# Layer norm and routing of the two expert stages taken block by block

## The reference

```python
x = x + 0.5 * ffn(layernorm(x))
x = x + mixer(layernorm(x))
x = x + 0.5 * ffn(layernorm(x))
x = x + 0.5 * moe(layernorm(x))
x = x + attention(layernorm(x))
x = x + 0.5 * moe(layernorm(x))

def moe(x):                      # 64 experts of 88 hidden rows, 8 used per token
    scores = sigmoid(x @ gate_w.T)
    choice = scores + gate_bias
    # sum of the 2 best of each of 8 groups; 4 best groups; 8 best experts in them
    w = scores where chosen, divided by their sum + 1e-20, times 2.5
    routed = sum_e w[:, e] * mlp_e(x)      # mlp: silu(x Wg.T) * (x Wu.T) @ Wd.T
    return routed + shared_mlp(x)          # 2 shared experts of 88 rows
```

## Time and profile before

| | us |
|---|---|
| median of three runs (lowest, highest) | 1801.06 (1800.49, 1803.01) |
| profiled execution, device time | 1803.61 |
| profiled execution, span of the trace | 1801.8 |
| PE, DVE, ACT, POOL busy in the span | 1614.6, 1234.6, 953.1, 902.6 |
| second feed-forward, from its first matmul | 495.4 to 648.5 |
| E1 up to the first weighted expert tile, E1 from there | 648.5 to 723.8, 723.8 to 1091.8 |
| attention: layer norm and first keys, then the heads | 1091.8 to 1114.6, 1114.6 to 1353.8 |
| E2 up to the first weighted expert tile, E2 from there | 1353.8 to 1431.9, 1431.9 to 1799.1 |

### The profile page before, as it was taken

The page is one execution under the profiler, slowest core; times in us unless marked ns, Lnnn a source line. Parts: engine busy times, 40 slices in busy tenths (PEclk is TensorE's granted clock), DMA queues, the critical chain, the costliest instruction groups (busy, mean ns, idle before and its releaser), DMA issues.

```text
span 1801.8 us, 25450 instructions
## 1 busy us (share of the span) xinstructions
PE 1614.6 (90%) x6820; PEld 1208.8 (67%) x6820; DVE 1234.6 (69%) x2015; ACT 953.1 (53%) x1864; POOL 902.6 (50%) x786
## 2 busy tenths in 40 slices
PE   5999558877799985999999997999998599999998
PEld 3777323333367763788888885988885488888887
DVE  4555779999945645666666666877775466666666
ACT  3234565444434342565555564877773265655565
POOL 2000147766610023677777773344433277777776
PEclk9999779999989986999999999999997799999999
DMA  2000000000000001676777760000000366767765
GB/s 111 1 0 1 0 0 1 0 0 1 0 8 1 0 35 37 143 154 144 157 147 149 151 138 1 2 0 0 0 1 9 76 152 145 155 146 154 149 149 119
DMA packets 30035, 118.72 MB, mean 66 GB/s; under 512 B 5323, under 2 KB 17059, under 8 KB 18211
## 3 DMA queue, kind: packets, MB, share of 16 engines
q1 hardware_dynamic: 29987, 118.15, 29.8%
HBM read 116.03 MB, written 2.10 MB: 66 GB/s over the span
## 4 chain that ended last, share of the span: by engine, by line
PE 65%; DVE 3%; issue 2%; POOL 2%; ACT 2%; DMA 1%; POOLq 0%; DVEq 0%; SPq 0%; ACTq 0%
PE ps L218 18%; PE ps L220 18%; PE ps L219 18%; PE ps L1270 2%; PE ps L1255 1%; PE ps L1257 1%; PE ps L1256 1%; POOL m_hc L831 1%; PE ps L621 1%; DMA rwb<-rw_rows 1%; PE ps L240 1%; POOL e_lo L226 1%; PE ps L253 1%; PE ps L1258 1%; DMA rw_rows<-rwt 0%
## 5 line engine op out<-in xcount | busy, mean ns | idle before, releaser
L226 POOL TENSOR_TENSOR e_lo<-e_h,e_hi 128x512 fp32r<-128x512 f32 (+1 forms) x368 | 479.0, 1302 | 258.3 <-ACT e_hi L223 251.2
L1138 DVE TENSOR_TENSOR ps<-e_s,ps 128x512 f32<-128x512 f32 x352 | 245.0, 696 | 237.8 <-PE ps L220 179.1
L963 ACT ACTIVATE e_s<-ps 128x512 f32<-128x512 f32 (+1 forms) x368 | 220.2, 598 | 323.6 <-PE ps L220 323.5
L218 PE MATMUL ps<-xn_hi,eh 128*128 128x512 f32 x704 | 280.4, 398 | 22.8 <-DVE ps L1138 22.8
L219 PE MATMUL ps<-xn_lo,eh 128*128 128x512 f32 x704 | 279.1, 396 | 0.0
L220 PE MATMUL ps<-xn_hi,el 128*128 128x512 f32 x704 | 278.1, 395 | 0.0
L1149 DVE TENSOR_TENSOR e_h<-ps,rwb 128x512 f32<-128x512 f32 x352 | 243.3, 691 | 44.9 <-DMA rwb<-rw_rows 21.3
L223 ACT ACTIVATE e_hi<-e_h 128x512 fp32r<-128x512 f32 (+1 forms) x368 | 229.0, 622 | 48.8 <-DVE e_h L1149 25.7
L831 POOL TENSOR_TENSOR m_hc<-m_h,m_c 128x512 f32<-128x512 f32 x128 | 172.8, 1350 | 126.6 <-DVE m_h L787 124.3
L226 POOL TENSOR_TENSOR xn_lo<-ln_c,xn_hi 128x512 fp32r<-128x512 f32 (+1 forms) x24 | 34.2, 1427 | 327.9 <-ACT xn_hi L223 327.8
L621 PE MATMUL ps<-m_hc,const 128*128 128x512 f32 x256 | 149.3, 666 | 48.7 <-POOL m_hc L831 43.7
(11 more groups left out here) (238 smaller groups left out, 3192.5 us busy)
## 6 DMA issues: line engine op xcount, KB each, us to landing
rwb<-rw_rows SPq DMA_DIRECT2D x32, 704.0 KB
rwb<-rw_rows SPq DMA_DIRECT2D x40, 512.0 KB
e_raw<-in_experts SPq DMA_DIRECT2D x88, 192.0 KB, 5.5
rwb<-rw_rows SPq DMA_DIRECT2D x16, 640.0 KB
rwb<-rw_rows SPq DMA_DIRECT2D x24, 384.0 KB
rwb<-rw_rows SPq DMA_DIRECT2D x16, 448.0 KB
rwb<-rw_rows SPq DMA_DIRECT2D x16, 320.0 KB
rwb<-rw_rows SPq DMA_DIRECT2D x40, 128.0 KB
```

Source lines behind the costliest of these rows:

```text
L218: pe.matmul(out, w_hi, x_hi, start=start, stop=False, skip_group_check=True)
L226: return eng.tensor_tensor(lo, full, hi.bitcast(F32), ALU.subtract)
L963: act.activation(e_s[0:rows_, buf, :], ps[0:rows_, 4, :], ACT.Silu).then_inc(S["silu"], 1)
L1138: dve.tensor_tensor(ps[0:rows_, 6 + buf % 2, :], e_s[0:rows_, buf, :], ps[0:rows_, 5, :], ALU.mult).then_inc(S["gated"], 1)
```

## The change

Each expert stage begins by blocks. The routing works on one block at a time (four token tiles, at most 128x256 elements) in 24 steps. They are cut into `route_pairs` (6), `route_groups` (6), `route_mask` (5), `route_top` (2, with 4 MAX8 and 4 MATCH_REPLACE8) and `route_weights` (5). PE issues 12 logit matmuls (`route_logits`) and 4 transposes (`route_turn`) for a block, ACT one sigmoid and one copy.

- **Second feed-forward.** Logits and sigmoid of blocks 0, 1 and 2 run in its blocks 1, 2 and 3. The routing of blocks 0 and 1 runs in its blocks 2 and 3, with the transposes and the copy.
- **Phase 3 (E1).** What is left is the layer norm of block 3 and the routing of blocks 2 and 3, written out beside the shared tiles.
- **Phase 5 (E2).** All four layer norms and routings are written out beside the shared tiles and the first expert tiles.
- **Tile order.** The first pair goes block by block (FIRST_TILES). In it the weighting reads and writes `e_h` in SBUF instead of passing through PSUM. The last pair ends in an order that finishes blocks 0 and 1 early (LAST_TILES).
- **DMAs.** A block's rows are written in two parts and read back by six DMAs of one block each. The rows of chunks 2 and 3 can be read only when tiles 6 and 7 of the first pair have been weighted. The weights of the two chunks of a later pair are loaded one behind the other, then their rows.
- **Attention.** Its weights are split in eight parts in pair 20. Its layer norm of blocks 0 and 1 runs in the last pair of E1, of blocks 2 and 3 beside the first heads. A second load of the attention weights is issued in E1 behind the rows of chunk 9.
- Feed-forward and attention blocks are written out instead of looped, and so are the first, the second last and the last pair.

```diff
+        def route_step(dve, R, b, k, ins):
+            ins.then_inc(R["route"], 1)
+            dve.wait_ge(*R("route", ROUTE_STEPS * b + k))
...
 in ffn_pe, block i, layer 2, before its third part:
+                        if R and i and layer_ == 1 and k == 2:
+                            route_logits(pe, R, N, i - 1, 0)
...
                         if k == 0:
                             pe.wait_ge(*L("xn_lo", i + 2))
+                            if R and i:
+                                pe.wait_ge(*R("scores", i))
+                        gate(i + 1, k)
                 last.then_inc(S["out"], 1)
+                if R and i >= 2:
+                    route_turn(pe, R, i - 2, 4)
...
 in ffn_dve, behind the splits of layers 1 and 2:
+                    if R and i >= 2 and layer_ == 1:
+                        route_pairs(dve, R, i - 2)
+                        route_groups(dve, R, i - 2)
+                        route_mask(dve, R, i - 2)
+                    if R and i >= 2 and layer_ == 2:
+                        route_top(dve, R, i - 2)
+                        route_weights(dve, R, i - 2)
...
+        FIRST_TILES = tuple((c, b) for b in range(NB) for c in range(2))
+        LAST_TILES = ((0, 0), (0, 1), (1, 0), (1, 1), (0, 2), (1, 2), (0, 3), (1, 3))
...
 moe_dve, E1 (E2 has the like, with four layer norms and four routings):
+            def one_block_left():
+                one_centre(dve, L, LAST, LAST)
+                route_pairs(dve, S, 2)
+                one_diagonal(dve, L, LAST)
+                route_groups(dve, S, 2)
+                shared_gate(0)
+                route_mask(dve, S, 2)
+                one_normalise(dve, L, LAST, LAST)
+                shared_gate(1)
+                shared_gate(2)
+                route_top(dve, S, 2)
+                shared_gate(3)
+                route_weights(dve, S, 2)
+                shared_gate(4)
+                route_pairs(dve, S, LAST)
...
+                route_top(dve, S, LAST)
+                first_tile(0)
+                route_weights(dve, S, LAST)
...
+            def first_tile(j):
+                c, b = FIRST_TILES[j]
+                t = in_pair(0, j)
...
+                dve.tensor_tensor(e_h[:, j % 4, :], e_s[:, j % 4, :], ps[:, 5, :], ALU.mult).then_inc(S["gated"], 1)
+                dve.wait_ge(*S("gated", t + 1))
+                if c == 0:
+                    dve.wait_ge(*S(f"rw_first{b}", 96))
+                dve.tensor_tensor(e_h[:, j % 4, :], e_h[:, j % 4, :], rwb[:, c, cut(b)], ALU.mult).then_inc(S["weighted"], 1)
...
+        def moe_first_rows(sp, S, b):
+            sp.wait_ge(*S("rwt", b + 1))
+            sp.dma_start(rw_rows[0:few, cut(b)], rwt[0:few, cut(b)]).then_inc(S[f"rw_few{b}"], 16)
+            sp.dma_start(rw_rows[few:E, cut(b)], rwt[few:E, cut(b)]).then_inc(S[f"rw_out{b}"], 16)
+            sp.wait_ge(*S(f"rw_few{b}", 16))
+            for ch in range(2):
+                for lo, hi, e in expert_rows(ch):
+                    sp.dma_start(rwb[lo:hi, ch, cut(b)], rw_rows[e:e + 1, cut(b)].broadcast_to([hi - lo, T])).then_inc(S[f"rw_first{b}"], 16)
...
             def row_weights(ch):
+                sp.wait_ge(*S("weighted", SHARED + NB * (ch - 1) if ch > 3 else SHARED + PER + ch - 3))
...
+            for ch in range(4, CH, 2):
                 weights(ch)
-                sp.wait_ge(*S("weighted", SHARED + NB * (ch - 1)))
+                weights(ch + 1)
                 row_weights(ch)
+                row_weights(ch + 1)
+                if S is E1 and ch == 8:
+                    sp.dma_start(a_raw[:, :], d["attn"]).then_inc(a_in, 16)
```

More of the change, by code:

```diff
@@ new lines, in route_scores, with route_turn @@
+        def route_scores(act, R, b, bank):
+            act.wait_ge(*R("logits", b + 1))
+            act.activation(r_s[:, b, :, :].rearrange("p t e -> p (t e)"), ps[:, bank, 0:4 * E], ACT.Sigmoid).then_inc(R["scores"], 1)
+        def route_turn(pe, R, b, bank):
+            pe.wait_ge(*R("route", ROUTE_STEPS * (b + 1)))
+            for t in range(4):
+                last = pe.transpose(ps[0:E, bank, t * P:(t + 1) * P], r_t[:, t * E:(t + 1) * E], ident)
+            last.then_inc(R["rw_t"], 1)
@@ L478, in ffn_pe, with ffn_act, block_ @@
                 pe.wait_ge(w_split, 4)
-            ffn_blocks(pe, block_)
-        def ffn_act(act, S, N):
-            def block_(i, blk, before, following):
+            for i in range(NB):
+                block_(i)
+        def ffn_act(act, S, N, R):
+            def block_(i):
+                if R and i == 1:
+                    moe_act(act, R)
                 for o in range(HC):
@@ L937, in moe_act @@
+            if N:
+                one_spread(pe, N, 1, 1)
         def moe_act(act, S):
@@ L940, in moe_act, with moe_act_tiles @@
             act.activation(sd_h[:, :, :], sd_raw[:, :, :], ACT.Identity).then_inc(S["small_hi"], 1)
-        def moe_act_tiles(act, S, attention):
-            load_table(act, ACT.Sigmoid)
-            for half in range(2):
-                act.wait_ge(*S("logits", half + 1))
-                act.activation(r_s[:, 8 * half:8 * half + 8, :].rearrange("p t e -> p (t e)"), ps[:, half, :], ACT.Sigmoid)\
-                    .then_inc(S["scores"], 1)
+        def moe_act_tiles(act, S, L, N):
             def gate_up_high(i, c, read):
@@ L1002, in moe_act_tiles @@
+                    if N and last and j >= 6:
+                        one_square(act, N, j - 6)
+            pair(0, False)
+            with act.Fori(1, PAIRS - 2) as i:
                 pair(i, False)
+            pair(PAIRS - 2, False)
             pair(PAIRS - 1, True)
+            if N:
+                one_deviation(act, N, 0, 0)
+                one_deviation(act, N, 1, 1)
+                one_high(act, N, 0)
+                one_high(act, N, 1)
         def moe_pool(pool, S):
@@ new lines, in moe_dve @@
+            if S is E1:
+                one_block_left()
+            else:
+                four_blocks_left()
+            dve.wait_ge(*S("rwt", NB))
+            with dve.Fori(1, PAIRS - 1) as i:
+                for j in range(PER):
+                    tile(i, j)
+            for j in range(PER):
+                tile(PAIRS - 1, j, LAST_TILES)
+                if j >= 5:
+                    x_new(j - 5)
+                if N and j >= 6:
+                    one_centre(dve, N, j - 6, j - 6)
@@ L1388, in heads @@
                         q_high(i + 1, 0)
+                    if i == 0 and h < 2:
+                        one_high(act, L, 2 + h)
                 output(i, HEADS - 1)
```

870 lines of the change are left out of this document (533 added, 337 removed).

## The result

Changed kernel: 1813.71 us median of 6 runs (1811.11 to 1817.40); the kernel before beside it: 1803.47 us (1800.49 to 1805.76). The ratio is 1.0059, 95% interval 1.0041 to 1.0077. The forecast of 1780 us and its range up to 1805 are missed, and the sign with them. The profiled execution of the changed kernel took 1811.63 us with a span of 1809.8, against 1803.61 and 1801.8.

A forecast was written before the change was run, and what follows sets the result against it. DVE's routing and the weights' way through DRAM, with PE standing still, were taken to bound the starts. E1 19.5, E2 -1, attention 4.5, code -1.5 gave 21.5 us off 1803.6: 1782 profiled, 1780 median, range 1757 to 1805.

The forecast's parts named there:

- Second feed-forward (term 11.9): Second feed-forward: moved logits, sigmoid waits and routing cost 11.9 us, bounds 5 and 18.
- Start of E1 (39.3 gained before deductions): Start of E1: a stretch of 75.3 us takes 36, with DVE as the bound.
- rows through DRAM: First pair and pair 1 of both expert stages: waits for expert rows cost 3 us in E1, 6.8 in E2.
- Start of E2 (term -1): Start of E2: gain 6.5 us, less 6.8 for rows and 1 for the DVE-ACT-POOL ring, makes -1.
- the walk of VectorE's work without a wait: Start of E2: from the first shared gate operation VectorE owes 48 us of work before tile 3 is weighted.
- The lock of VectorE and GpSimd: Both expert starts: 0.6 us lost per GpSimd split beside routing, about 5 us in E1 and 7 in E2.
- second rival: Expert starts: GpSimd comes first nearly every time, each split blocks 1.26 us; near 1802 us, 1810 with slow landing; chance 0.17.
- My two signs of being wrong: Wrong if E2's start shrinks by over 10 us, or if the feed-forward grows by over 18.
- E1's end and attention (4.5, less 1.5 for code): E1's tail to attention's scores: gain 5.5 us less 1 for table loads, 4.5; written-out loops take 1.5.
- Written-out code: Written-out loops: 1.5 us taken for instructions fetched once more, though no row shows a cost.
- Clock: Start of E1: 2 us deducted because the clock may again run at 0.50, while the walk uses full speed.
- third rival: Both expert starts: the clock falls, adding 9 us in E1 and 3 in E2, for 1792 us; chance 0.15.

The follow-up runs named there:

- transposes_free: Changed kernel with the last routing step writing over the block's scores, so transposes read that tile instead of the shared one; 1806.84 us, ratio 1.0023.
- short_gpsimd_splits: Changed kernel with GpSimd's low-part subtraction covering only 16 of 512 columns for the 16 tiles of E2's start; 1802.13 us, ratio 0.9988.
- norm_before_heads: mended_and_routed_at_once with attention normalising blocks 2 and 3 wholly before its first query; 1789.43 us, ratio 0.9934.
- second_stage_routed_at_once: transposes_free with E2 routing all four blocks in one pass of 24 steps over 1024 elements; 1805.54 us, ratio 1.0007.
- mended_and_routed_at_once: Changed kernel with transposes mended, separate row buffer, last pair's rows early, one attention-weights load, six experts in the short write, E2 routed in one pass; 1788.10 us, ratio 0.9910.

## Why the prediction was wrong

**Second feed-forward (term 11.9): right.** The last update comes 12.1 us later, and without the routing there 12.3 come back.

**Start of E1 (39.3 gained before deductions): nearly right.** From the update of x to pair 1 it takes 64.9 us instead of 92.6, a gain of 27.7; I had 32.3. The step that failed is "rows through DRAM". I took 6 us for the landing of a chunk's rows from the earlier trace rows and so 3 us of stall. Chunk 2's go out together with chunk 3's, 2 MB in all, and took 9.1 to 9.5 us; the stall was 7.40. A buffer of their own took 3 us off each stage's stall and won 8.5 us. Whether it is the second megabyte that makes them slow was not tried: no run issues them alone. A second step was missing altogether: 1.88 us of wait for the transposes.

**Start of E2 (term -1): measured -17.** It is 16 us short, 6.5 before tile 3 is weighted and 9.5 behind it.
- *Up to tile 3* the failed step is the walk of VectorE's work without a wait: 48 us from the first shared gate operation, where 56.2 passed (1370.71 to 1426.88). 8.0 of these are waits, 3.54 and 2.81 for the transposes, which were nothing in my sum, and 1.63 for a product of TensorE. The first shared gate operation itself came 2.4 us earlier in the stage than I had it. So tile 3, to be weighted 6.5 us earlier than before, came at 1426.88, 83 us after the stage began, as before. transposes_free won 6.5 us in both stages together.
- *Behind tile 3* the failed step is "rows through DRAM". To pair 1 it takes 28.0 us (10.7 before), 17.3 more where I had 7.8. At tile 6 I took a wait of 5.4, of which 4.2 was to reach TensorE, and it was 6.82; for pair 1's rows I took 2.6, and it was 7.14.
- *The lock of VectorE and GpSimd* did not fail: 7 us, 0.6 per split, was my term, and 8.2, 0.5 per split, went from VectorE's instructions in short_gpsimd_splits. Those 11 to 13 us are what there was to win from the lock and shorter splits, and most of it was in my sum already. Of the second rival's two conditions, a mean block of 1.1 us did not come, though single instructions lost 0.8 to 1.1; a landing of 9 us did.
- The last pair's rows, some 2 us in each stage: nothing in my sum.

My two signs of being wrong both stayed away: E2's start did not shrink by 10 us, it grew, and the feed-forward grew by 12. Neither would have shown this outcome.

A chain of routing with 24 short steps per block costs VectorE 43.7 us, locks included, where one pass costs 26 to 31; I had priced that. E1 won with two of its four blocks routed elsewhere. In E2 block by block lost 10 us to the one pass once the other waits were mended (105.2 against 95.6); for E1 no run shows that part by itself.

**E1's end and attention (4.5, less 1.5 for code): measured -2.9.** The first minimum did come 3.1 us earlier against E1's last gate operation, where I had 4.5. The failed step is one that I did not take: I counted the norm of blocks 2 and 3 as gone from the front and didn't charge it where it went, between the first two heads: 4.2 us up to block 0's update, and norm_before_heads takes 3.8 of them away. Written-out code was 1.8 and not shown to be the cause.

**Clock** (2 us in E1): not needed there, it ran at 0.91, where the start before had 0.70. The third rival's low clock did not come in E1; in E2 the clock was as before, 0.77 for 0.76.

## What to carry to other kernels

Work moved beside other work is paid twice, in the fixed part of every shorter instruction and in the locks that short instructions meet; in E2 halves gave a better trade than quarters and, at the edge of what the runs resolve, than one pass. When a serial way through DRAM is cut into blocks, add up what its queue then does in series (5 us a block here), and ask which transfers are issued together. Every wait in the diff gets a line in the sum, those that guard a scratch tile above all.

## What the runs showed that I had not expected

The same layer norm at the start of E2 gets different clocks in different profiles, by no part of the program that I could name. In its first 16 us the first line is second_stage_routed_at_once, the second mended_and_routed_at_once, which have the same instructions there:

```profile
1343.50:1359.50 16.00, 16.00 (x41) 9.68 (x42) 6.69 (x12) 3.93 (x8) 1.27 (x1) 0.52 0.00 1
```

```profile
1338.20:1354.20 16.00, 14.63 (x63) 8.84 (x63) 8.02 (x15) 6.13 (x12) 2.53 (x2) 0.82 0.00 1
```

At 0.52, near the lower level of 1.2 GHz, TensorE is busy throughout and the first routing step begins 32.4 us after attention's last update; at 0.82 it begins after 26.6. In both TensorE was at the upper level, 2.4 GHz, while it was busy nearly all of the time, and then it was busy only 3.3 to 3.8 of the 6.5 us before that update. In mended_and_routed_at_once the clock fell just before the update and was up again 4 us behind it (0.50, then 0.95 in the next 4 us). In second_stage_routed_at_once it fell just behind the update and stayed at 0.50 for some 24 us. norm_before_heads has these instructions too and got 0.60 in the 16 us behind the update, with pair 1 after 98.3 us instead of 95.6. That is 6 us in a single profile, as much as most edits here, and a reason to compare stages from an event behind it and totals by several timed runs.
